# Row attention: context as high and low values side by side, exponential in two instructions, scores bank by bank

## What is computed

```python
q = (x @ Wq + bq).reshape(B, S, NH, dh)      # S = 1250, NH = 8, dh = 64
k = (x @ Wk + bk).reshape(B, S, NH, dh)
v = (x @ Wv + bv).reshape(B, S, NH, dh)
scores = jnp.einsum('bqhd,bkhd->bhqk', q, k) / jnp.sqrt(jnp.float32(dh)).astype(x.dtype)
attn = jax.nn.softmax(scores, axis=-1)
ctx = jnp.einsum('bhqk,bkhd->bqhd', attn, v).reshape(B, S, D)
sa = ctx @ Wo + bo
x = _layernorm(x + sa, g1, beta1)
# then: expert of the largest gate logit for each row, its two layers, a last layernorm
```

## Time and profile before

| | |
|---|---|
| median of the runs shown | 1955.11 us (1953.63 to 1959.61, 3 runs) |
| profiled execution | 1956.35 us, span 1954.7 us from the first to the last instruction |
| mean granted TensorE clock | 0.960 of full speed |
| busy in the span | PE 1777.9 us (91%), DVE 1314.1 (67%), ACT 907.0 (46%), POOL 590.2 (30%) |

### The profile page before, as it was taken

The page is one execution under the profiler, slowest core; times in us unless marked ns, Lnnn a source line. Parts: engine busy times, 40 slices in busy tenths (PEclk is TensorE's granted clock), DMA queues, the critical chain, the costliest instruction groups (busy, mean ns, idle before and its releaser), DMA issues. The chain is left out here.

```text
span 1954.7 us, 31926 instructions
## 1 busy us (share of the span) xinstructions
PE 1777.9 (91%) x10958; PEld 1544.2 (79%) x10958; DVE 1314.1 (67%) x2945; ACT 907.0 (46%) x1652; POOL 590.2 (30%) x531
## 2 busy tenths in 40 slices
PE   7998969899999999898679999999899999999496
PEld 5776769888888888676567998988688888888385
DVE  5444336688888888378664565645578787886676
ACT  4332236677777776222131234324365555555421
POOL 0000030365555652111100021122254545444244
PEclk9999989999999999899889999999999999999698
DMA  6652495677777775656233027976010211113432
GB/s 239 210 187 86 144 302 194 188 207 203 202 201 203 200 204 141 157 142 153 72 106 92 1 84 151 198 207 210 19 33 17 58 31 32 31 32 120 160 120 87
DMA packets 183532, 265.14 MB, mean 136 GB/s; under 512 B 55852, under 2 KB 102443, under 8 KB 181109
## 3 DMA queue, kind: packets, MB, share of 16 engines
q1 hardware_dynamic: 117839, 169.58, 29.9%
q0 software_dynamic: 49920, 62.94, 12.1%
q10 hardware_dynamic: 15640, 30.90, 6.5%
HBM read 198.55 MB, written 85.86 MB: 145 GB/s over the span
## 5 line engine op out<-in xcount | busy, mean ns | idle before, releaser
L1063 POOL DMA_INDIRECT edge_rows<-xn_store,edge_index x200 | 245.2, 1226 | 254.1 <-PE psum L138 104.3
L2539 POOL TENSOR_TENSOR mprob<-mprob,mrden 125x1250 f32<-125x1250 f32 x80 | 181.7, 2273 | 218.4 <-DVE mrden L2645 218.0
L2568 ACT ACTIVATE mprob<-psum,mbias 125x1250 f32<-125x1250 f32 x80 | 104.4, 1305 | 153.4 <-DVE mbias L2654 153.4
L1279 DVE TENSOR_TENSOR edge_xt_lo<-psum,edge_xt_hi 128x500 fp32r<-128x500 f32 x200 | 134.8, 675 | 52.6 <-ACT edge_xt_hi L1156 52.6
L2652 DVE TENSOR_REDUCE mmin<-psum 125x1 f32<-125x512 f32 (+1 forms) x240 | 126.8, 583 | 47.7 <-PE psum L2811 47.5
L1156 ACT ACTIVATE edge_xt_hi<-psum 128x500 fp32r<-128x500 f32 x200 | 117.8, 590 | 87.8 <-PE psum L1442 87.8
L2829 PE MATMUL psum<-ident,mprob 125*125 125x125 f32 x800 | 117.9, 292 | 18.6 <-DVE ptm_lo L2659 9.4
L2829 PEld LDWEIGHTS psum<-ident,mprob 125*125 125x125 f32 x800 | 100.3, 191 | 36.2 <-DVE ptm_lo L2659 20.2
L2659 DVE TENSOR_TENSOR ptm_lo<-psum,ptm_hi 125x500 fp32r<-125x500 f32 (+1 forms) x240 | 126.3, 581 | 2.0 <-ACT ptm_hi L2574 2.0
L1442 PE MATMUL psum<-ident,edge_rows 125*128 125x125 f32 x800 | 120.0, 273 | 3.7 <-DVE edge_xt_lo L1279 2.0
L1308 DVE TENSOR_TENSOR edge_rows_lo<-edge_rows,edge_rows_hi 125x1024 fp32r<-125x1024 f32 x100 | 121.1, 1211 | 0.0
(11 more groups left out here) (519 smaller groups left out, 5370.4 us busy)
## 6 DMA issues: line engine op xcount, KB each, us to landing
slots_in<-blank_rows ACTq DMA_DIRECT2D x20, 1026.0 KB, 16.2
t_store<-t_part SPq DMA_DIRECT2D x20, 1000.0 KB, 5.3
t_row<-t_store SPq DMA_DIRECT2D x47, 400.0 KB, 6.8
y_store<-y_rows SPq DMA_DIRECT2D x50, 200.0 KB
q_chunk<-q_store SPq DMA_DIRECT2D x40, 250.0 KB, 5.4
y_tile<-y_store SPq DMA_DIRECT2D x10, 896.0 KB
edge_attr<-in_attr SPq DMA_DIRECT2D x50, 112.0 KB
moe_xg<-slots_in SPq DMA_DIRECT2D x17, 256.5 KB, 3.5
```

The source lines that it names most:

```text
L1063: nc.gpsimd.indirect_dma_start(xe[t % RING][:, s, :], None, g.xn_store, bass.IndirectOffsetOnAxis(ap=index[t % RING][:, s, 0:1], axis=0)). ...
L1279: nc.vector.tensor_tensor(xt_lo[:, k, :], x_bank(KT * t + k), f32(xt_hi[:, k, :]), ALU.subtract).then_inc(x_low, 1)
L2539: nc.gpsimd.tensor_tensor(prob[:, n % 4, :], prob[:, n % 4, :], rden[:, n % 4:n % 4 + 1].broadcast_to([P, N]), ALU.mult).then_inc(p_ready, 1)
```

## The change

The values of a head are kept as high and low part side by side (`v_both`): for each pair of heads four blocks of 64 columns, in the order high and low of the even head, low and high of the odd head. One matmul with the 128 columns of a head gives its high part's product in the rows of that head and its low part's product in the other 64 rows. So `context` has two matmuls for each key tile, with the high and the low probabilities, in place of three. ScalarE copies the other 64 rows out as `ctx_rest`, ahead of `ctx_hi`, and `output` adds a fourth matmul for each k, `ctx_rest` by `wo_hi`. As `ctx_rest` lies where the raw output weights were, ScalarE waits for `wo_ready` in step 6 of chunk 0. The exponential is made in two instructions, columns 0 to 511 (the first bank) and 512 to 1249, each with its own sum in `mden` and its own raise of `e_ready`. `inverse` waits for both, adds the two sums and takes the reciprocal of the result. `scores` waits for the first exponential of the step before ahead of the first bank and for the second ahead of the second bank.

```diff
-CREDITS = {"at_e_ready": 1, "at_tp_free": 3, "at_c_free": 1, "at_summed": 1, "moe_placed": 1, "moe_scattered": 1}
+CREDITS = {"at_e_ready": 2, "at_tp_free": 3, "at_c_free": 1, "at_summed": 1, "moe_placed": 1, "moe_scattered": 1}
 class Core:
...
     g.k_stack = at("k_stack", [128, NH, N], F32R, 12)
-    g.v_hi, g.v_lo = at("v_hi", [P, NT, D], F32R, 132), at("v_lo", [P, NT, D], F32R, 152)
+    g.v_both = at("v_both", [P, NT, KT, 4, DH], F32R, 132)
     g.qs = at("q_chunk", [128, 2, NH, CH], F32R, 112)
...
     kv_hi = [at(f"kv_w_hi{i}", [128, KT, D], F32R, kb) for i, kb in enumerate((116, 156, 172))]
...
     ctx_hi, ctx_lo = at("ctx_hi", [128, KT, CH], F32R, 196.25), at("ctx_lo", [128, KT, CH], F32R, 200.25)
+    ctx_rest = at("ctx_rest", [128, KT, CH], F32R, 192.125)
     wo_hi, wo_lo = at("wo_hi", [128, KT, D], F32R, 172), at("wo_lo", [128, KT, D], F32R, 180)
     pt = [(at("ptm_hi0", [P, NT, CH], F32R, 52), at("ptm_lo0", [P, NT, CH], F32R, 62)),
...
     low = at("mmin", [P, 2, 4], F32, S)
-    bias, den, rden = (at(n, [P, 4], F32, S + .125 + i / 16) for i, n in enumerate(("mbias", "mden", "mrden")))
+    bias, rden = (at(n, [P, 4], F32, S + .125 + i / 16) for i, n in enumerate(("mbias", "mrden")))
+    den = at("mden", [P, 2, 4], F32, S + .25)
+    EXPS = (slice(0, SPANS[0][1]), slice(SPANS[0][1], N))
...
     g1, beta1 = at("moe_g1", [P, D], F32, 204.25), at("moe_beta1", [P, D], F32, 10)
...
     def piece(q):
...
         return core.bank(3 + q)[0:P, 0:(j1 - j0) * P].rearrange("p (j n) -> p j n", n=P)
+
+    def values_of(t, half):
+
+        slots = (slice(0, 4, 3), slice(1, 3))[half]
+        return g.v_both[:, t, :, slots, :]
+
+    def by_head(ap):
+        return ap.rearrange("p (k i d) -> p k i d", k=KT, i=2)
     def place(n):
...
             def exponentials(n):
                 act.wait_ge(m_ready, sub.step())
-                nc.scalar.activation(prob[:, n % 4, :], score[:, 0:N], ACT.Exp, bias=bias[:, n % 4:n % 4 + 1],
-                                     scale=-1.0, accum_out=den[:, n % 4:n % 4 + 1]).then_inc(e_ready, 1)
+                for i, cols in enumerate(EXPS):
+                    nc.scalar.activation(prob[:, n % 4, cols], score[:, cols], ACT.Exp, bias=bias[:, n % 4:n % 4 + 1],
+                                         scale=-1.0, accum_out=den[:, i, n % 4:n % 4 + 1]).then_inc(e_ready, 1)
             def turned_hi(n):
                 for q, (j0, j1) in enumerate(PIECES):
...
             def context_hi(hh):
...
                 act.wait_ge(c_done, ctx.step())
+                nc.scalar.activation(ctx_rest[rows_, k, :], ctx_bank[place(2 * hh + 2)[0], 0:CH], ACT.Copy)
                 nc.scalar.activation(ctx_hi[rows_, k, :], ctx_bank[rows_, 0:CH], ACT.Copy).then_inc(c_hi, 1)
             def weights_1(experts):
...
                             act.wait_ge(v_summed, t + 1)
-                            nc.scalar.activation(g.v_hi[:, t, :], vsum[:, t % 2, :], ACT.Copy).then_inc(v_top, 1)
+                            nc.scalar.activation(values_of(t, 0), by_head(vsum[:, t % 2, :]), ACT.Copy).then_inc(v_top, 1)
+                    if n == 6 and isinstance(c, int) and c == 0:
+                        act.wait_ge(wo_ready, 1)
                     if n % 2 == 0 and live(n - 6):
...
                     if live(n - 2):
...
             def value_lo(t):
                 dve.wait_ge(v_top, t + 1)
-                nc.vector.tensor_tensor(g.v_lo[:, t, :], vsum[:, t % 2, :], f32(g.v_hi[:, t, :]), ALU.subtract).then_inc(v_low, 1)
+                nc.vector.tensor_tensor(values_of(t, 1), by_head(vsum[:, t % 2, :]), f32(values_of(t, 0)), ALU.subtract).then_inc(v_low, 1)
             def inverse(n):
-                dve.wait_ge(e_ready, 1 + exps.step())
-                nc.vector.reciprocal(rden[:, n % 4:n % 4 + 1], den[:, n % 4:n % 4 + 1]).then_inc(r_ready, 1)
+                dve.wait_ge(e_ready, 2 + exps.step(2))
+                own = slice(n % 4, n % 4 + 1)
+                link(nc.vector.tensor_tensor(rden[:, own], den[:, 0, own], den[:, 1, own], ALU.add))
+                nc.vector.reciprocal(rden[:, own], rden[:, own]).then_inc(r_ready, 1)
             def maximum(n):
...
-            chunks(dve, chunk, ((spans, 3 * SUBS), (exps, SUBS), (tp, 3 * SUBS), (ctx, NH), (link, SUBS + 2 + 13 + 5 + 6)))
+            chunks(dve, chunk, ((spans, 3 * SUBS), (exps, 2 * SUBS), (tp, 3 * SUBS), (ctx, NH), (link, 2 * SUBS + 2 + 13 + 5 + 6)))
             mix.vector(dve, lambda: [lower_2(i) for i in range(EARLY, NE)])
         @block.tensor
...
             def scores(n):
                 cols = place(n)[2]
-                pe.wait_ge(e_ready, exps.step())
-                for a, b in SPANS:
+                before = exps.step(2)
+                for q, (a, b) in enumerate(SPANS):
+                    if q < 2:
+                        pe.wait_ge(e_ready, before - 1 + q)
                     for half in range(2):
...
                                                 start=half == 0, stop=half == 1)
...
                 for j in range(half * NT // 2, (half + 1) * NT // 2):
-                    last = three_pass(nc, ctx_bank[:, 0:CH],
-                                      [x[:, j, 128 * (hh // 2):128 * (hh // 2) + 128] for x in (g.v_hi, g.v_lo)],
-                                      [x[:, j, :] for x in pt[hh % 2]], j == 0, j == NT - 1)
+                    own = g.v_both[:, j, hh // 2, 2 * (hh % 2):2 * (hh % 2) + 2, :].rearrange("p i d -> p (i d)")
+                    for i, probs in enumerate(pt[hh % 2]):
+                        last = nc.tensor.matmul(ctx_bank[:, 0:CH], own, probs[:, j, :], start=j == i == 0, stop=j == NT - 1 and i == 1)
                 if half == 1:
...
                 for k in range(KT):
-                    last = three_pass(nc, gate_bank[0:P, :],
-                                      [x[:, k, s * P:(s + 1) * P] for x in (ctx_hi, ctx_lo)],
-                                      [x[:, k, :] for x in (wo_hi, wo_lo)], k == 0, k == KT - 1)
+                    three_pass(nc, gate_bank[0:P, :], [x[:, k, s * P:(s + 1) * P] for x in (ctx_hi, ctx_lo)],
+                               [x[:, k, :] for x in (wo_hi, wo_lo)], k == 0, False)
+                    last = nc.tensor.matmul(gate_bank[0:P, :], ctx_rest[:, k, s * P:(s + 1) * P], wo_hi[:, k, :], start=False,
+                                            stop=k == KT - 1)
                 last.then_inc(o_done, 1)
             def turn_rows(c, s):
...
-            chunks(pe, chunk, ((exps, SUBS), (sub, SUBS), (tp, 3 * SUBS), (ctx, NH)))
+            chunks(pe, chunk, ((exps, 2 * SUBS), (sub, SUBS), (tp, 3 * SUBS), (ctx, NH)))
             mix.tensor(pe)
```

## The result

The changed kernel took 1977.7 us (median of 4 runs, 1972.7 to 1982.0), the kernel before beside it on the same chip 1957.4 us (4 runs, 1953.6 to 1959.8): a ratio of 1.0105, with an interval of 1.0073 to 1.0136. It is slower, by 20.3 us where 13.4 was forecast, and its time lies 0.7 us above the end of the range. Two later sets gave 1970.9 against 1955.5 and 1973.2 against 1957.4, ratios of 1.0082 and 1.0090, that is 15.4 and 15.8 us more. The profiled execution took 1972.7 us (span 1971.1), 16.4 us more than that of before. It was the shortest of the four, 5.0 us under their median.

A forecast was written before the change was run, and what follows sets the result against it. Bound by a loop of TensorE and VectorE, not TensorE's work: chunks 1 to 4 9.9, chunk 0 0.4, copies 3.0, tail 0.1, together +13.4 on 1955.1, so 1968.5 us; range 1957.5 to 1977.

The forecast's parts named there:

- the loss at the copies: Steps with a context copy: ScalarE's longer chain makes VectorE's minima late by 0.12 us, 25 times, 3.0 us.
- the split of the exponential: ScalarE: two instructions cost nothing themselves; the second accumulator read adds 0.12 us, bounds 0 and 0.30.
- What bounds the kernel: Row attention: a loop of TensorE and VectorE, 4.42 us a step; transposes wait for `ptm_lo` behind the minima.
- Context in two passes, worth nothing in plain steps: TensorE: 0.585 us less per half head, 46.8 us busy time; plain steps no shorter, transposes wait 0.8 instead of 0.2.
- The output's fourth pass: TensorE, steps 5 and 6 of chunks 1 to 4 and the tail: four more matmuls per row tile, 0.93 us.
- The sum of periods 5 and 6, 1.48: Minima of step 7 come later by 0.35 + 0.93 + 0.20 (inverse), 1.48 us in each of chunks 1 to 4.
- The 0.35 of period 5: Step 5, set by TensorE: 0.93 of output less 0.585 of context makes the next scores 0.35 us later.
- The addition in `inverse`: VectorE, ahead of the minima: 0.20 us where minima don't wait for scores (28 steps), hidden in plain steps.
- The bound of 0.30: Upper bound for the exponential's split on ScalarE: a read, and a start that waits for it, 0.30 us.
- The clock: Rival: TensorE idle 0.8 us in every plain step lowers its granted clock to 0.91, +29 us, 1997 us; 7%.
- the sign of 0.97: Sign that the forecast is wrong: a granted clock under 0.97 between 1440 and 1800 us.
- VectorE and ScalarE swallow their additions: Rival: only the output passes count, 5.2 us, 1960.4 us; 15% together with other outcomes inside 0.3%.

The follow-up runs named there:

- Filling the holes: Changed kernel with five unused matmuls of 250 columns added to each half head of the context, in all steps but the output's; ratio 1.0093.
- The context's part alone: Kernel before with only the context in two passes, the copy `ctx_rest` and the output's fourth matmul, one exponential; ratio 1.0047.
- the exponential's alone: Kernel before with only the exponential in two instructions, the addition in `inverse` and the scores' wait by bank; ratio 1.0045.
- each half alone: Kernel before with one half of the diff: two-pass context, `ctx_rest` and fourth output matmul, 1.0047; or exponential in two, addition and scores by bank, 1.0045.
- the other order: Kernel before with `ptm_lo`'s first piece ahead of VectorE's minima in even steps and `inverse` behind `ptm_lo` in all steps; ratio 1.0152.

## Why the forecast came out as it did

The mechanism was right, and the step that failed is a term of the sum: the loss at the copies, put at 3.0 us, measured 4.4, because the split of the exponential was put at 0.12 us and takes 0.26. Beside it stand terms put at nothing, the clock behind the gates and the additions held by GpSimd. These account for the stage; some 4 us of the first set stay open.

- **What bounds the kernel** was right. Plain periods without a copy are 4.42 us before and after; with a third of the context's matmuls gone they are 4.42 to 4.47; with the first piece moved they are 4.03 to 4.10. The idle time of the weight loads of the transposes went from 0.2 to 0.8 us, as forecast, that of the transposes themselves to 0.6.
- **Context in two passes, worth nothing in plain steps:** right. Its one gain, 0.58 us in period 5, came as computed.
- **The output's fourth pass:** 0.93 us right. The sum of periods 5 and 6, 1.48, was too high; it was 1.17. The 0.35 of period 5 starts from minima that the copies had already made late, and I added what overlaps. Four chunks: 1.2 us too much.
- **The addition in `inverse`:** right, 0.20 (0.19 to 0.24) in the steps named. Hidden in plain steps: right, but for one case that I had not thought of, where it stands beside GpSimd's product. Over seven profiles of kernels with this addition the one in period 1 of chunks 2 to 4 lasted 0.22 to 1.62 us instead of 0.16; in the profile after this cost 0.4 us in all, in the one with `ctx_hi` first 0.6 and 0.7 us in two chunks.
- **The copies:** this term of the sum was mis-sized. The split of the exponential was put at 0.12 us; it takes 0.26 (1.67 less 1.41). I had taken the split itself as free and charged part of the second read of the accumulator. The timeline has it the other way round: the two parts last 0.69 and 0.87 us, 1.56 together, where the whole took 1.30, while the first read lies wholly under the two parts. The other links were right: 0.38 for the copy (0.40 taken), 0.40 to `ctx_lo`, 0.34 or 0.46 to the minima. So the minima start 2.79 us (heads in the lower half) or 2.91 us (upper half) after the exponential. Less 2.60 that is a loss of 0.19 or 0.31, and the periods show 0.12 to 0.16 and 0.27 to 0.30. The number of such periods was too high: 21, not 25, as period 10 of chunks 1 to 4 stayed at 4.85 us. That was luck, since 25 would have cost 0.8 us more. Measured 4.4 us, not 3.0. The bound of 0.30 that I kept for the range was the right end. "Copies of 500 columns follow one another without a loss" was the wrong row to lean on; that they write no accumulator may be the difference, which no run shows. The rule quoted from the Trainium skill, stated of VectorE, agrees with what ScalarE shows here: the new copy holds up `ctx_hi` for 0.38 us in both kinds of head.
- **The clock:** from chunk 1 on the plain steps of the profile after kept a granted clock of 1.00, but for one behind the gates (period 14 of chunk 1), and 1440 to 1800 us had 0.98 (1.00 before), above the sign of 0.97. So this rival fails at the size that I gave it, and the rule of the Trainium skill on short idle times isn't borne out here at idle times of 0.6 to 0.8 us. But stretches of a low clock stood behind the gates of all four chunks in two profiles of the changed kernel and three of four in the third, against one before. The 5 us from 1710, at 0.50, are wholly at the lower level, 1.2 GHz. Each cost up to 1.1 us. Whether the change causes them isn't shown. Filling the holes removed one of them and won no time; and the kernel with two of three matmuls, whose transposes wait as long (53.4 us), has them in one chunk only, like the kernel before. The context's part alone has them in three chunks, the exponential's alone in one.
- **VectorE and ScalarE swallow their additions:** false by the runs with each half alone.
- **The sum.** 13.3 us for the stage against 13.8, 14.0 and 16.0 in three profiles. The differences from the forecast are +1.4 (copies), -1.2 (overlap), +0.35 (periods 7 to 9, 12 and 13), +0.6 (chunk 0), and in the profile of the first set 1.5 of clock and held addition. The third and fourth are mostly the clock again: the addition by itself was right to 0.1 us for each chunk. That the errors of the terms partly cancel is luck too. The rest of the 20.3 us of the first set, some 4 us, isn't in the stage of any profile, and the execution profiled was the shortest of its set. The interval of that set begins at 14.3 us, those of the other two (11.5 to 20.7 and 12.3 to 22.9 us) hold the forecast. Why the first set lies above them stays open. Of the 9.2 us between 1968.5 and 1977.7, 2.3 are that the kernel before took 1957.4 and not 1955.1 beside it, and the times of the two later sets lie inside the range. The range was too narrow on that side: it took in the costs' bounds and nothing for a mechanism not in the trace of before, nor for how far sets of runs differ.

## What to carry to other kernels

An engine that is 96% busy need not be the bound. It isn't where each of its groups starts on another engine's signal: follow one step in the timeline and see which start has no idle time before it; taking work off that engine pays only there. Where a chain on a second engine lies within a few tenths of a microsecond of the loop, two harmless additions to it can cost together what neither costs alone, so cost them together. A cheaper step may be to move work into the wait, as the first piece of `ptm_lo` ahead of the minima did.

## What the runs showed of the hardware

- A VectorE operation with two inputs in SBUF that starts while GpSimd multiplies in SBUF lasted until the product's end: 2.27 instead of 0.16 us for two numbers for each partition (the kernel before with the other order), 1.26 for one (the changed kernel). The form with a per-partition scalar (0.21 us) and reciprocals (0.16 us) weren't held.
- Splitting one exponential of 1250 columns with a sum into 512 and 738 delays what follows on ScalarE by 0.26 us: the parts last 0.69 and 0.87 us, the whole 1.30. Each read of the accumulator takes 0.19 to 0.20 us; the one between the parts starts 0.10 us before the first ends and ends 0.10 us after the second starts.
- TensorE, idle 0.6 to 0.8 us in every 4.4 us, kept a granted clock of 1.00 in the plain steps, but for one that stood right behind a step with gates.
